# A decoder block on one core: the value projections of a head move into the next step, between its successor's keys and queries

## What is computed

```python
q = causal_conv_silu(x @ Wq);  k = causal_conv_silu(x @ Wk);  v = causal_conv_silu(x @ Wv)   # conv of 4 taps
q, k = l2norm(q) / sqrt(128), l2norm(k)          # two k and two v per token and head
beta = 2 * sigmoid(x @ Wb);  g = -exp(A_log) * softplus(x @ Wa + dt_bias)
for t in tokens:
    state *= exp(g[t])
    for j in range(2):
        u = (v[t, j] - k[t, j] @ state) * beta[t, j]
        state += outer(k[t, j], u)
    o[t] = q[t] @ state
x += (rmsnorm(o) * norm_w * silu(x @ Wg)) @ Wo
# 2: similarities of ctx, per row a threshold at the 76th largest value, a mask, a mix with layernorm(x)
# 3: a base MLP and 8 experts, two chosen per token
```

## Time and profile before

| | |
|---|---|
| median of 3 runs | 935.14 us (933.33 to 941.7) |
| profiled execution: its time, its span | 941.6 us, 939.8 us |
| granted clock of PE, mean | 0.905 |
| busy: PE, DVE, ACT, POOL | 841.2, 519.8, 422.1, 344.9 us |
| attention (steps 0 to 10) | to about 632 us of the span |
| step 0 (projections begin at 20.0) | to 64.1 |
| step 1, step 2 | 65.3, 68.5 us |
| steps 3 to 7 | 64.7, 64.6, 64.6, 63.8, 65.7 us |
| step 8 | 73.6 us |
| steps 9 and 10 | 32.3 us and 5 us |

### The profile page before, as it was taken

The page is one execution under the profiler, slowest core; times in us unless marked ns, Lnnn a source line. Parts: engine busy times, 40 slices in busy tenths (PEclk is TensorE's granted clock), DMA queues, the critical chain, the costliest instruction groups (busy, mean ns, idle before and its releaser), DMA issues. The chain is left out here.

```text
span 939.8 us, 16187 instructions
## 1 busy us (share of the span) xinstructions
PE 841.2 (90%) x5500; PEld 610.6 (65%) x5501; DVE 519.8 (55%) x1259; ACT 422.1 (45%) x929; POOL 344.9 (37%) x654
## 2 busy tenths in 40 slices
PE   4767999899999999999999876975999999999992
PEld 3333486686786776866867765864667667676761
DVE  3664638778887897887888655466411111111113
ACT  2656757456655656656666234213222222222220
POOL 1127466357368456564673480003420000000015
PEclk9879969879989899799899777796999999999997
DMA  7504133123150141141201301009673100110104
GB/s 187 141 25 111 23 85 90 24 59 67 24 121 5 38 109 21 31 98 24 56 19 24 89 2 29 2 1 366 238 241 109 33 24 32 33 33 22 33 24 128
DMA packets 107362, 66.30 MB, mean 71 GB/s; under 512 B 64864, under 2 KB 98720, under 8 KB 107296
## 3 DMA queue, kind: packets, MB, share of 16 engines
q1 hardware_dynamic: 99904, 59.52, 24.0%
q0 software_dynamic: 1536, 4.20, 1.5%
q10 hardware_dynamic: 5856, 1.73, 0.8%
HBM read 50.84 MB, written 14.58 MB: 70 GB/s over the span
## 5 line engine op out<-in xcount | busy, mean ns | idle before, releaser
L1129 DVE SCALAR_TENSOR_TENSOR y<-bank,cwh,y 128x510 f32<-128x510 f32 (+2 forms) x240 | 177.1, 743 | 57.9 <-ACT y L883 53.7
L633 PE MATMUL bank<-xnT,wbuf 128*128 128x512 f32 x320 | 163.0, 635 | 7.3 <-DVE y L1129 7.3
L1668 PE MATMUL bank<-f_wgu,f_xgT 128*128 x368 | 118.8, 466 | 0.0
L1946 DVE TENSOR_TENSOR f_act<-f_sg,bank 128x352 f32<-128x352 f32 x62 | 32.2, 521 | 143.8 <-PE bank L1668 141.5
L1433 POOL TENSOR_TENSOR term<-inv,blk 128x126 f32<-128x126 f32 (+22 forms) x248 | 87.8, 354 | 57.9 <-DMA blk<-a_blocks 39.1
L1785 ACT ACTIVATE f_sg<-bank 128x352 f32<-128x352 f32 x62 | 28.7, 464 | 161.1 <-PE bank L1668 152.7
L633 PEld LDWEIGHTS bank<-xnT,wbuf 128*128 128x128 f32 x320 | 57.9, 199 | 66.4 <-issue 53.8
L2021 POOL DMA_INDIRECT f_back<-slots_y,f_slot x16 | 15.4, 963 | 231.5 <-DMA slots_y<-f_yb 224.9
L1436 POOL TENSOR_TENSOR inv<-inv,term 128x126 f32<-128x126 f32 (+22 forms) x248 | 91.5, 369 | 19.4
L1713 PE MATMUL bank<-f_wdn,f_actT 128*128 (+1 forms) x372 | 91.5, 388 | 1.0 <-ACT f_actT L1798 0.8
L1668 PEld LDWEIGHTS bank<-f_wgu,f_xgT 128*128 128x128 f32 x368 | 66.2, 190 | 36.8 <-issue 7.6
(11 more groups left out here) (209 smaller groups left out, 1537.4 us busy)
## 6 DMA issues: line engine op xcount, KB each, us to landing
f_wgu<-in_exp_gu SPq DMA_DIRECT2D x8, 1408.0 KB, 9.7
f_wdn<-in_exp_dn SPq DMA_DIRECT2D x8, 640.0 KB, 10.5
dr<-sums SPq DMA_DIRECT2D x16, 256.0 KB, 4.5
ex<-sums SPq DMA_DIRECT2D x16, 256.0 KB, 4.5
blk<-a_blocks SPq DMA_DIRECT2D x16, 256.0 KB, 4.0
slots_x<-oT SPq DMA_DIRECT2D x24, 128.0 KB, 1.9
f_xg<-slots_x SPq DMA_DIRECT2D x24, 128.0 KB, 2.0
slots_y<-f_yb SPq DMA_DIRECT2D x23, 128.0 KB, 1.7
```

What stands on the lines that cost most here:

```text
L633: last = mm(bankA[p % 2][:, :], wbuf[A.par][:, kt, wblk, :], xnT[:, kt, (p % 2) * 512:(p % 2 + 1) * 512], start=kt == 0, stop=kt == 1)
L1129: v.scalar_tensor_tensor(out=y[p % 2][:, :, k:], in0=src[:, :, 0:SEQ - k], scalar=cwh[A.par][:, cb, 3 - k:4 - k], in1=y[p % 2][:, :, k:], ...
L1668: last = mm(gu[c][:, 0:FFH], xt[:, k, :], wgu[:, e, k, at:at + FFH], start=k == 0, stop=k == 1)
L1946: v.tensor_tensor(av[:, par, half * FFH:(half + 1) * FFH], sg[:, half, :], gu[2 * half + 1][:, 0:FFH], ALU.mult).then_inc(f_act, 1)
```

## The change

**Projections.** A table `PROJECTION` gives the order: slots 0 to 3 the keys of A, slots 4 to 7 the values of B, slots 8 and 9 the queries of A. So step 0 has six projections, and step 8, where A is empty, four. Waits that counted ten projections a head now count by the table (`nth`).

**Items.** `vtok` moves from slots 1, 2, 3, 5 to slots 9 (two), 10 and 11; the gates from 4 and 9 to 3 and 5. The squares of the queries move from slots 9 and 10 to 11, their norms on PE behind `x32`.

**Exponentials.** Those of head 0 stand at the end of slot 11 in step 0, those of head 1 at the end of slot 8 in step 1; the exponentials of the gate's sums (`scalar_decays`) go with the first.

**Loads.** Weights of values are loaded apart, one head later. Of the zero writes 4 stay ahead of step 0, 20 stand in step 1 between the differences' rows and `scatter`; the gate's weights follow `scatter` there. POOL copies a head's taps (`cwh`) a step earlier.

**Selection.** In step 8 the two tiles are cut into fours and twos over slots 1 to 8, with ten instructions behind the slots.

```diff
 FILL = {FIRST: {"B": [("pair", n) for n in range(BC // 2)]},
-        1: {"E": [("out", 0)], "B": [("vtok", 0)]},
-        2: {"B": [("vtok", 1)]},
-        3: {"B": [("vtok", 2)]},
-        4: {"E": [("out", 1)], "B": [("gate", 0)]},
-        5: {"B": [("vtok", 3)]},
+        1: {"E": [("out", 0)]},
+        3: {"B": [("gate", 0)]},
+        4: {"E": [("out", 1)]},
+        5: {"B": [("gate", 1)]},
         6: {"B": [("kend", 0)]},
...
-        9: {"B": [("kend", 2), ("gate", 1)]},
-        10: {"B": [("p32", 0), ("p32", 1)], "E": [("out", 3)]},
-        11: {"B": [("t32", 0), ("t32", 1)]},
+        9: {"B": [("kend", 2), ("vtok", 0), ("vtok", 1)]},
+        10: {"B": [("p32", 0), ("p32", 1), ("vtok", 2)], "E": [("out", 3)]},
+        11: {"B": [("t32", 0), ("t32", 1), ("vtok", 3)]},
...
-SCALARS_AT = 3
-EXP_AT = {0: 7, 1: 2}
+SCALARS_AT = 2
+EXP_AT = {0: 11, 1: 8}
+
+def projection(slot, A, B):
+    X, p = (A, slot) if slot < 4 else (B, slot + 2) if slot < 8 else (A, slot - 4)
+    return (X, p) if X else None
...
@@ sync_program, step
+            if A and A.h:
+                value_weights(A.h)
...
             if A and A.h < HEADS - 1:
                 difference_rows(A.h + 1)
+            if s == 1:
+                zero_slots(4, SLOT_TILES)
             if B:
                 scatter(B)
...
@@ tensor_program, step
-                if A and slot < 10:
-                    proj(A, slot)
-                if A and slot == 11:
-                    norm(A, 4)
+                if slot < 10 and projection(slot, A, B):
+                    proj(*projection(slot, A, B))
             fill(BLOCKS_64)
             if A:
+                norm(A, 4)
                 norm(A, 5)
...
@@ scalar_program, step
-                if slot == EXP_AT.get(s, -1):
-                    decays(A)
-                    pair_decays(A)
-                if s == HEADS and slot == 7:
+                if 2 <= slot and projection(slot - 2, A, B):
+                    silu(*projection(slot - 2, A, B))
+                if s == HEADS and slot == 9:
                     sigmoids()
-                if A and 2 <= slot:
-                    silu(A, slot - 2)
-                if A and 5 <= slot <= 10:
+                if A and 5 <= slot <= 8:
                     square(A, slot - 5)
-                if A and slot < 10:
-                    evac(A, slot)
+                if A and slot == 11:
+                    square(A, 4)
+                    square(A, 5)
+                if slot < 10 and projection(slot, A, B):
+                    evac(*projection(slot, A, B))
+                if slot == EXP_AT.get(s, -1):
+                    exp_table()
+                    pair_decays(A)
+                    decays(A)
+                    if s == 0:
+                        scalar_decays()
...
@@ vector_program, step
-                if not A and tiles and slot == 5:
-                    topk(tiles[0], 8, 2 * ROUNDS)
+                if not A and tiles and 1 <= slot <= 3:
+                    topk(tiles[0], 4 * slot + 4, 4 * slot + 8)
+                if not A and tiles and 4 <= slot <= 8:
+                    topk(tiles[1], 2 * slot - 8, 2 * slot - 6)
                 if not A and tiles and slot == 9:
                     gamma_parts()
-                    topk(tiles[1], 0, 2 * ROUNDS)
...
+            if not A and tiles:
+                topk(tiles[1], 10, 2 * ROUNDS)
```

More of the change, by code:

```diff
@@ L121, with projection_table, nth @@
 B_BANKS = 3
-SCALARS_AT = 3
-EXP_AT = {0: 7, 1: 2}
+SCALARS_AT = 2
[3 more added lines that the diff above has]
+    return (X, p) if X else None
+def projection_table():
+    out = []
+    run_heads(lambda A, B, C, E: out.extend(projection(slot, A, B) for slot in range(10)))
+    return {(x[0].h, x[1]): i for i, x in enumerate(x for x in out if x)}
+PROJECTION = projection_table()
+def nth(h, p):
+    return PROJECTION[h, p] + 1
 def items_at(place):
@@ L361, in attention @@
     w_in = [w_in0, w_in1]
+    wv_in = [sem(f"wv_in{i}") for i in range(2)]
     wo_in = [wo_in0, wo_in1]
@@ L443, in sync_program, with zero_slots @@
         sp.wait_ge(zero_done, 1)
-        for m in range(SLOT_TILES):
-            sp.dma_start(dram["slots_x"][m], zero).then_inc(slots_zeroed, 16)
-        for k in range(KT_H):
-            sp.dma_start(gwT[:, k, :], dram["gate_w"].rearrange("e (k p) -> k p e", p=P)[k], allow_slow_non_contiguous=True).then_inc(mix_in, 16)
+        def zero_slots(first, end):
+            for m in range(first, end):
+                sp.dma_start(dram["slots_x"][m], zero).then_inc(slots_zeroed, 16)
+        zero_slots(0, 4)
         blocks = a_blocks.rearrange("(p x) -> p x", x=NB * NB)
@@ L1299, in step @@
                     gate_ends()
-                if A and 1 <= slot <= 10:
-                    conv(A, slot - 1, (1,))
+                todo = projection(slot - 1, A, B) if 1 <= slot <= 10 else None
+                if todo:
+                    conv(*todo, (1,))
                 if C:
                     scan(C, slot)
-                if A and 1 <= slot <= 10:
-                    conv(A, slot - 1, (2, 3))
+                if todo:
+                    conv(*todo, (2, 3))
                 fill(slot)
@@ L1340, in gpsimd_program, with taps @@
         pool.wait_ge(small_in, 160)
-        def start(A):
-            h = A.h
-            if not isinstance(h, int) or h >= 2:
-                if some(30 * (h - 1)):
-                    pool.wait_ge(conv_step, 30 * (h - 1))
-            g.tensor_copy(cwh[A.par][:, :, :].rearrange("p a k -> p (a k)"),
+        def taps(h):
+            if h >= 2:
+                pool.wait_ge(conv_step, 3 * nth(h - 2, 9))
+            g.tensor_copy(cwh[h % 2][:, :, :].rearrange("p a k -> p (a k)"),
                           cw[:, :, :, :].rearrange("p h a k -> p h (a k)")[:, h, :]).then_inc(cwh_done, 1)
@@ L1441, in step @@
                 unit(B)
[L1442 to L1443 removed]
             if A and A.h == 0:
+                taps(0)
+                taps(1)
                 clear(A)
```

83 lines of the change are left out of this document (51 added, 32 removed).

## The result

| | before | after |
|---|---|---|
| median, runs of one comparison | 936.29 us (933.33 to 941.7) | 953.34 us (947.9 to 959.16) |
| ratio, with 95% interval | | 1.0176 [1.0098, 1.0255] |
| the same comparison on another occasion | 931.14 us | 949.68 us, 1.0195 [1.0112, 1.0277] |
| profiled execution: its time, its span | 941.6, 939.8 us | 954.75, 952.9 us |
| granted clock, mean | 0.905 | 0.892 |

A forecast was written before the change was run, and what follows sets the result against it. PE was not the only bound: a loop through inversion, transfer, turn and products takes the same 64.6 us. Terms -11.9 + 9.5 + 3.5 + 3.7 + 10.5 - 3.1 = +12.2 us gave 947.3 on the median, range 929 to 957.

The forecast's parts named there:

- Step 0, -11.9: Step 0: with six projections instead of ten, the last scaled blocks come at 59.3 instead of 71.24, 11.9 us earlier.
- The switch of tables: ACT, steps 0 and 1: a table load costs 1.30 us by the rows, not the skill's 2.66; seven switches become five.
- Step 1, +9.5 and +3.5: Step 1: SP's zero writes hold the solved blocks, +9.5 us to the turn; the tail runs at 1.2 GHz, +3.5.
- Step 2, +3.7: Step 2: +2.7 us for its tail and +1.0 for similarities leaving SP later.
- the term for similarities that leave late: Step 2: similarities leave SP after the gate weights and later-ending query decays, +1.0 us.
- Steady tail, +2.1 a step: Steps 3 to 7: value evacuation, activation and squares on ACT delay the 64-block products 2.1 us each, +10.5 in all.
- PE is ahead by the two value turns, and waits for the turn instead: Tail: nothing becomes shorter in return, as PE arrives earlier by two value turns and waits for the turn.
- the clock falls earlier: Rival, chance 0.10: the tail at 0.50 throughout takes 19.3 us instead of 16.1, 3.2 more in five steps: 963.
- Step 8, -3.1: Step 8: cut selections bring the turn 5.1 us earlier, two value turns on PE add 2.0; sum -3.1.
- SP is not held: Rival, chance 0.13: in step 1 head 1's pair exponential comes before about 84 us, so the 9.5 falls away: 937.8.
- the tail stays as it was: Rival, chance 0.14: ACT's added work is hidden or products start before it; 2.1 us fall away in seven steps: 932.6.
- the value turns keep the clock up: Rival, chance 0.06: the clock stays up through the 64 products, giving back up to 3 us a step: 932.

The follow-up runs named there:

- e4: Changed kernel with two unused 512-column matmuls on PE just ahead of the 32-block products in steps 1 to 7; ratio 1.0214 to the kernel before.
- e5: Changed kernel with step 1's twenty zero writes ahead of SP's wait for the pair exponential instead of behind it; ratio 1.0118 to the kernel before.
- e7: Changed kernel with head 0's exponentials at slot 7 instead of 11 and head 1's at slot 4 instead of 8; ratio 1.0047 to the kernel before.
- e2: Changed kernel with the last two value turns ahead of the 32-block products in slot 10 instead of behind them; ratio 1.0096 to the kernel before.
- b1_selection: Kernel before with only step 8's second-tile selection spread over DVE's slots 4 to 8 and the end; ratio 0.9943 to the kernel before.
- e1: Changed kernel with step 1's twenty zero writes moved behind head 0's solved blocks and head 2's decay rows on SP; ratio 1.0206 to the kernel before.
- b2: Kernel before with only both query squares at slot 11 on ACT and their column sums later on PE; ratio 1.0088 to the kernel before.
- e6: Changed kernel with zero writes in SP's idle time, two value turns ahead of p32, one square at slot 10, step 8's turn before gate parts; ratio 0.9912.

## Why the prediction was right, and where it was not

**Step 0, -11.9: mechanism right, and the number by luck.** The early starts give -11.7, but the prediction was worked out from the rows of a late one, and there the change gives -14.3. Set beside e4, which has the changed step 0 and a late start: the second query projection leaves DVE at 46.5 and not at 48.0, the chain behind it on ACT and POOL takes the 4.1 us that the sum had to the fold's start, and the scaled blocks follow each other in 4.5 us and not 5.1. So the last ones start at 57.1 where I had 59.3, and at 53.6 in the profiled execution; my window of 58 to 61 was missed in every run. I also took the profiled execution of before for the measure, though it stood 6.5 us above the median (941.6 against 935.1). Its late start can be 5.3 of that. With it taken out, the two profiles differ by 13.9 + 5.3 = 19 us at the end of step 8, near the 17 of the medians.

**The switch of tables: the row was right.** 84.81 to 86.10 is 1.29 us again. The traces have seven loads from 20 us to the end of step 1 before and five after, as the prediction counted. No run shows the larger price.

**Step 1, +9.5 and +3.5: right, mechanism and size** (+9.7, +3.2). The exponential came at 86.1 and not at 91.6, since step 0 was shorter, but the inversion ended 5.0 us earlier too, and the difference stayed. The prediction's window for the zero writes, 90 to 96, was missed by 2 us for that reason. Both cuts of the chain (e5, e7) give the turn back.

**Step 2, +3.7: mis-sized,** +1.9. Its tail grew by 2.0 (18.5 to 20.5) where I had 2.7; the term for similarities that leave late found nothing.

**Steady tail, +2.1 a step: right in mechanism, wrong in its parts.** x32 to p64 grew by 1.8 in the steps where the clock stayed up, less than the 2.1. But p32 to t32 grew too, from 3.9 to 4.3 even at the full clock: the value turn of PE in slot 10, which the prediction called covered by PE's earlier arrival, is not covered, since PE stands waiting when it arrives. In the two steps without a low clock behind the wait, 4 and 5, the step is 65.73 and 65.84 us, +1.1 and +1.2; I had said about 66.7. In e7's execution two such steps are at 64.8. What comes back is that p64 to t64 sometimes runs at full clock (2.0 instead of 3.0 us), and that pairs to turn is up to 1 us shorter.

**The step that failed: "PE is ahead by the two value turns, and waits for the turn instead".** I gave that wait no price in the sum. It was the rival "the clock falls earlier", at 0.10, as a tail at 0.50 throughout in all five steps. It came in three of the five: steps 3, 6 and 7 are 73.7, 69.2 and 69.1 us, 9.0, 5.3 and 3.4 above before. The pieces from the turn to the pairs grew by 19.4 us in the five steps, which is nearly all of the +20.0. Of this, x32 to p64 is 8.5, the term that I had at 10.5; p32 to t32 is 8.8, of which the value turn makes 2.1 and the low clock in three steps the other 6.7; the rest, t32 to x32 above all, is 2.1. The time at 0.50 in steps 3 to 7 rose from 47 to 74 us (79 in the other execution). The filler (e4) and the early value turns (e2) took the wait away or cut it to 1.0 us and less, and no step had the low clock in p32 to t32 any more.

That 953.3 lies in the range was not foreseen either. The rival with the clock stood at 963 and the range, which ended at 957, left most of it out. The time stayed inside because the clock fell in three steps and not in five. The Trainium skill (TensorE: Matmul & The Clock Gate, Part 1), which I had cited for that rival, calls the slow clock the default that activity releases. The falls behind the waits agree with it. In the tail the clock is also low while PE is busy throughout (0.51 over 6.47 us), in the kernel before as well, and why is open.

**Step 8, -3.1: right** (-3.3), part by part: from pairs to turn 54.3 to 48.9 us, -5.4 where I had -5.1, although the turn waited for the sigmoid's result and stands 7.1 us behind the inversion, 0.7 more than in b1_selection; the tail 19.2 to 21.3, +2.1 where I had +2.0.

**The rivals that lost.** "SP is not held" needed the exponential 10 us ahead of the inversion's end, and it came 2.9 ahead (86.10 against 88.98); "the tail stays as it was" and "the value turns keep the clock up" had no row for them: the value turns behind p32 run at the low clock like the rest (1.11 us in step 3 instead of 0.66).

## To carry to other kernels

A transfer that nobody waits for costs its issue time to whatever stands behind it in the queue: read the queue on to its next user and the one after it, also when you repair it (e1 moved 9 us into the next step, e5 removed them). Work taken from in front of a wait on PE is not free even when the wait was there anyway, since a wait lengthened by a microsecond or two can halve the clock of the work behind it (behind 14 of 20 such waits here). And before a profile's total is set against a median, look whether the profiled execution is a typical one: here 5 us of the difference lay in the first 64.

## What was not expected of the hardware

- The same instructions at the start of an execution take one of two times, by when PE's clock rises. In the kernel before the matmuls of the first projections start 0.85 us apart up to 23.6 us and 0.43 us apart behind it, a factor of two as between the two levels, 1.2 and 2.4 GHz. In b1_selection they are 0.43 us apart from the first. Line of the projections in the kernel before, up to 23.4 us and from 24.2 us on, then in b1_selection from 17.5 to 23 us (duration in ns, shortest, median, longest; first and last start):

```profile
L633 PE MATMUL bank<-xnT,wbuf x4: 1061/1061/1222, 20.0 to 22.7; 128*128 128x512 f32 x4
```

```profile
L633 PE MATMUL bank<-xnT,wbuf x4: 592/592/697, 23.6 to 25.0; 128*128 128x512 f32 x4
```

```profile
L633 PE MATMUL bank<-xnT,wbuf x8: 592/592/697, 18.1 to 21.2; 128*128 128x512 f32 x8
```

- The profile's view does not tell this. It gives a granted clock of 1.00 from 17 to 18 us in both. But the first record of the clock in the trace begins at 23.8 us in the kernel before and at 14.9 in b1_selection, and the view counts what lies ahead of the first record as full speed. A clock read at the start of a trace has to be checked against the spacing of the matmuls.
- Of fourteen profiled executions, four had the late start (before, b2, e4, e6; first record of the clock at 23.1 to 23.9 us), ten the early one (14.9 to 16.1 us). By the last scaled blocks it costs 5.3 us in the kernel before and 2.7 in the changed one. What makes the clock rise later in some executions stays open.
- Waits of PE of only 1.2 to 1.8 us, in a step in which it is otherwise busy, were followed by the low clock in most cases and not in all; the same kernel lost it in different steps in two executions.
